# Attention division with heads on partitions, a 128-row projection, and the second biases on GpSimd

## The reference

```
x = x + leaky(sum_e combine_e * (groupnorm(x) @ We_e + be_e))       # 2 of 5 experts
t = tokens(x)                                                       # 16 sequences of 256
q, k, v per head (6 heads of 16), causal softmax(k q / sqrt(96)) v  # -> heads
t = t + heads @ wproj + bproj
w = top-2 softmax weights of (layernorm(t) @ gate_w + gate_b)       # 4 experts, renormalised
t = t + sum_e w_e * (gelu(layernorm(t) @ w1_e + b1_e) @ w2_e + b2_e)
```

## Time and profile before

| what | value |
|---|---|
| median of 3 runs | 353.42 us (352.49 to 353.59) |
| the profiled execution, its own time | 352.74 us |
| span of its trace, first to last instruction | 351.0 us |
| PE busy | 335.9 us, 96% |
| DVE busy | 231.2 us, 66% |
| ACT busy | 231.8 us, 66% |
| POOL busy | 107.8 us, 31% |
| mean granted TensorE clock | 0.988 of full speed |

### The profile page before, as it was taken

How to read it: one execution, slowest core, us unless ns; L and a number is a source line. 1 busy time by engine, 2 the same in 40 slices (tenths; PEclk the granted TensorE clock), 3 DMA queues, 4 the chain that set the end, 5 groups by cost and what they waited for, 6 DMA issues and landing times.

```text
span 351.0 us, 7705 instructions
## 1 busy us (share of the span) xinstructions
PE 335.9 (96%) x2627; PEld 273.5 (78%) x2627; DVE 231.2 (66%) x1025; ACT 231.8 (66%) x467; POOL 107.8 (31%) x179
## 2 busy tenths in 40 slices
PE   6889998879999999999999999999999999999995
PEld 3655466546788987789878988898799789889895
DVE  4859895977379789868686698747647623453232
ACT  3777873555779689548864866497916977374460
POOL 3457761535432224043340434303410305001000
PEclk9999999889999999999999999999999999999999
DMA  7800018452300023013025000500230000000000
GB/s 189 168 4 0 2 35 102 76 63 57 82 3 1 4 67 92 2 52 89 22 69 69 4 23 25 114 5 22 80 57 4 25 2 2 24 1 2 22 2 23
DMA packets 24123, 14.80 MB, mean 42 GB/s; under 512 B 14323, under 2 KB 24083, under 8 KB 24084
## 3 DMA queue, kind: packets, MB, share of 16 engines
q1 hardware_dynamic: 22740, 13.13, 17.0%
q10 hardware_dynamic: 1344, 1.18, 2.7%
HBM read 3.10 MB, written 1.57 MB: 13 GB/s over the span
## 4 chain that ended last, share of the span: by engine, by line
PE 77%; DVE 6%; ACT 6%; DMA 4%; POOL 2%; ACTq 2%; issue 2%; SPq 1%; DVEq 0%; POOLq 0%
PE PS L994 24%; PE PS L787 10%; PE PS L789 9%; PE PS L788 9%; DMA k_stack<-qk_parts 4%; PE PS L931 4%; PE PS L889 3%; PE PS L913 3%; PE PS L840 2%; PE PS L955 2%; PE PS L800 2%; ACTq L684 2%; PE PS L988 2%; PE PS L878 1%; PE PS L940 1%
## 5 line engine op out<-in xcount | busy, mean ns | idle before, releaser
L994 PEld LDWEIGHTS PS<-w_f,hidden 128*128 128x128 f32 x768 | 90.0, 192 | 0.1
L994 PE MATMUL PS<-w_f,hidden 128*128 128x96 f32 x768 | 90.0, 274 | 0.0
L780 ACT ACTIVATE hidden<-PS 128x512 f32<-128x512 f32 x96 | 54.9, 596 | 29.5 <-PE PS L789 27.5
L1234 DVE SCALAR_TENSOR_TENSOR res<-PS,weight,res 128x96 f32<-128x96 f32 x128 | 31.7, 311 | 48.3 <-PE PS L994 48.2
L1152 DVE CUSTOM_DVE_ANT_0 masked<-PS,causal 128x128 bf16<-128x128 f32 (+1 forms) x120 | 35.1, 353 | 9.5 <-PE PS L878 7.4
L787 PE MATMUL PS<-t_hi,w_hi 97*128 97x512 f32 x96 | 40.9, 426 | 0.0
L800 PE MATMUL PS<-ones_b 128*128 128x512 bf16 x153 | 37.0, 391 | 3.4 <-POOL ones_b L518 3.4
L789 PE MATMUL PS<-t_hi,w_lo 97*128 97x512 f32 x96 | 38.1, 397 | 0.0
L788 PE MATMUL PS<-t_lo,w_hi 96*128 96x512 f32 x96 | 38.1, 397 | 0.0
L622 POOL TENSOR_SCALAR_AFFINE_SELECT prob_a<-prob_a 128x768 f32<-128x768 f32 x16 | 13.9, 866 | 65.5 <-ACT prob_a L742 65.5
L1113 DVE SCALAR_TENSOR_TENSOR PS<-conv_y,weight,PS 128x96 f32<-128x96 f32 x128 | 30.3, 315 | 5.1 <-ACT PS L694 5.0
(11 more groups left out here) (170 smaller groups left out, 703.9 us busy)
## 6 DMA issues: line engine op xcount, KB each, us to landing
q_stack<-qk_parts SPq DMA_DIRECT2D x48, 96.0 KB, 3.2
k_stack<-qk_parts SPq DMA_DIRECT2D x36, 96.0 KB, 3.4
out_dram<-res SPq DMA_DIRECT2D x8, 192.0 KB, 2.2
k_stack<-qk_parts ACTq DMA_DIRECT2D x12, 96.0 KB, 5.9
X<-in_x_dram SPq DMA_DIRECT2D x4, 192.0 KB, 2.9
X<-in_x_dram SPq DMA_DIRECT2D x2, 384.0 KB, 5.2
hidden<-in_L_ffn_w_dram SPq DMA_DIRECT2D x1, 576.0 KB
w_f<-in_L_ffn_w_dram SPq DMA_DIRECT2D x1, 576.0 KB
```

Of the source, the lines that this page charges most:

```text
L780: act.activation(hidden[:, m, 0:T * P], PS[:, bank("ffn1", n, index), 0:T * P], ACT.Gelu).then_inc(act_emptied["ffn1"], 1)
L994: mm = pe.matmul(PS[:, y, t * C:(t + 1) * C], hidden[:, m, t * P:(t + 1) * P], w2_f[:, m, :], start=False, stop=t == T - 1 and c == CHUNKS ...
L1234: ins = dve.scalar_tensor_tensor(res2[:, t, :], PS[:, y, t * C:(t + 1) * C], weight1[:, t, e:e + 1], res2[:, t, :], ALU.mult, ALU.add).the ...
```

## The change

Five things change.

1. The division is done on `pv`'s own layout. DVE copies each head's sum (row 16 of its 32) to all 32 rows of the group with a stream shuffle, takes the reciprocal of the whole tile, and multiplies: for a unit the step `att.0` on 512 columns and `att.1` on 256. The steps `out_t` and `heads_t` and ACT's copies of `pv` and `heads_t` are gone.
2. `proj` multiplies the 128 rows directly, with `wproj` laid out in the same groups of 32 rows, zeros between: each of the four token tiles takes two matmuls, one for the round of four heads and one for the round that holds two heads of each image. The bias sits at row 16 of the first group, where a sum times its reciprocal is one. `pv`'s third list of heads changes so that the shared round is the middle one.
3. The matmuls of `b2` are gone from `ffn2`. POOL has a new step `bias`: for each of the four experts a multiplication of the broadcast bias with the weights (128x384) and an addition into the residual, each waiting for the one before. It starts after `weights` and `norm2`; the first `ffn2` addition of DVE waits for it.
4. The loads change: `wproj` in four strided pieces, `b2` broadcast to 128 partitions, `bproj` to one row; 11 instead of 10.
5. `ORDER` is rewritten throughout, with 152 instead of 153 `warm` matmuls in 19 instead of 15 places.

```diff
     PE: """
-        conv.3@3:2 warm.7@9:6 norm1_t@1:6 warm.17@10:4 conv.0@4:4 conv.1@4:0 conv.2@4:3 v@1:1 qk.0@1:2 qk.1@1:5
+        conv.2@2:6 conv.3@2:0 warm.21@8:2 norm1_t@0:2 warm.3@9:4 conv.0@3:4 conv.1@3:3 conv.2@3:5 qk.0@0:1 qk.1@0:6
...
+        wproj_r = sb("wproj_r", [P, 3, C])
+        b2_rows = sb("b2_rows", [P, E1, C])
+        bias_e = sb("bias_e", [P, TILES, C])
...
+                elif kind == "bias":
+                    weight1, res2 = weight1s[n % WEIGHTS], res2s[n % RES2]
+                    shape = [P, T, C]
+                    if n == 0:
+                        pool.wait_ge(ffn_loaded, 16 * FFN_LOADS)
+                    pool.wait_ge(weight1_ready, n + 1)
+                    pool.wait_ge(normed_ready[1], tile0 + T)
+                    wait_dve(pool, "proj", n)
+                    for e in range(E1):
+                        if n > 0 or e > 0:
+                            pool.wait_ge(bias_added, E1 * n + e)
+                        pool.tensor_tensor(bias_e[:, 0:T, :], b2_rows[:, e, :].unsqueeze(1).to_broadcast(shape),
+                                           weight1[:, 0:T, e].unsqueeze(2).to_broadcast(shape), ALU.mult).then_inc(bias_ready, 1)
+                        pool.wait_ge(bias_ready, E1 * n + e + 1)
+                        pool.tensor_tensor(res2[:, 0:T, :], res2[:, 0:T, :], bias_e[:, 0:T, :], ALU.add).then_inc(bias_added, 1)
...
                             for j in range(HG):
-                                image, h = divmod(HG * r + j, HEADS)
+                                image, h = ((0, j), (j // 2, HG + j % 2), (1, j))[r]
...
-                    wait_act(pe, "heads_t", n)
-                    for t in range(T):
-                        mm = pe.matmul(PS[:, bank("proj", n), t * C:(t + 1) * C], heads_t[:, t * P:(t + 1) * P],
-                                       wproj_f[:, :], start=True, stop=True)
+                    wait_dve(pe, "pv", n, (1,))
+                    for image in range(W):
+                        for half in range(2):
+                            t, rows = 2 * image + half, slice(half * P, (half + 1) * P)
+                            pe.matmul(PS[:, bank("proj", n), t * C:(t + 1) * C], att_t[:, 2 * image, rows], wproj_r[:, 0, :],
+                                      start=True, stop=False)
+                            mm = pe.matmul(PS[:, bank("proj", n), t * C:(t + 1) * C], att_t[:, 1, rows],
+                                           wproj_r[:, 1 + image, :], start=False, stop=True)
...
-                    pe.matmul(PS[:, y, 0:T * C], ones_b[:, :],
-                              b2_parts[:, e * C:(e + 1) * C].unsqueeze(1).to_broadcast([P, T, C]),
-                              start=True, stop=False, skip_group_check=True)
...
+                elif kind == "att":
+                    r = index[0]
+                    rounds = (slice(0, 2), slice(2, ROUNDS))[r]
+                    width = (rounds.stop - rounds.start) * TOKENS
+                    heads = PS[:, bank("pv", n, index), 0:width]
+                    wait_filled(dve, "pv", n, index)
...
+                    step_done(dve.stream_shuffle(sums[:, 0:width], heads, [D] * HS))
                     wait_step()
+                    step_done(dve.reciprocal(sums[:, 0:width], sums[:, 0:width]))
+                    wait_step()
+                    if n > 0:
+                        wait_filled(dve, "proj", n - 1)
+                    dve.tensor_tensor(att_t[:, rounds, :].rearrange("p r t -> p (r t)"), heads, sums[:, 0:width],
+                                      ALU.mult).then_inc(dve_emptied["pv"], 1)
...
                     wait_filled(dve, "ffn2", n, index)
+                    if e == 0:
+                        dve.wait_ge(weight1_ready, n + 1)
+                        dve.wait_ge(bias_added, E1 * (n + 1))
```

More of the change, by code:

```diff
@@ L58 @@
[L58 to L72, removed]
@@ L73 @@
-        ffn1.7@1:3 out_t.0@2:1 out_t.1@2:4 score.1.1@3:5 score.1.2@3:6 score.1.3@3:0 score.1.4@3:3 qk.0@4:2 qk.1@4:1
-        heads_t@2:4 ffn1.8@1:5 ffn1.9@1:6 ffn1.10@1:4 ffn1.11@1:0 ffn2.0@1:5 proj@2:6 shift@3:3 v@4:4 ffn2.1@1:0
-        ffn2.2@1:2 prob.0.0@3:1 conv.0@7:5 norm2_t@2:3 ffn2.3@1:4 prob.0.1@3:6 prob.0.2@3:0 prob.0.3@3:1 prob.0.4@3:5
-        norm1_t@5:2 prob.1.0@3:3 prob.1.1@3:6 prob.1.2@3:0 conv.1@7:4 gate2@2:1 prob.1.3@3:5 prob.1.4@3:3
-        score.0.0@4:6 ffn1.0@2:0 ffn1.1@2:5 ffn1.2@2:3 ffn1.3@2:1 qk.0@5:4 qk.1@5:2 ffn1.4@2:6 pv.0@3:0 score.0.1@4:5
@@ L83 @@
-        ffn2.3@2:0 gate2@3:6 norm1_t@6:4 score.1.0@5:3 pv.0@4:5 pv.1@4:2 score.1.1@5:1 ffn1.0@3:0 out_t.0@4:6
-        out_t.1@4:5 ffn1.1@3:4 qk.0@6:2 score.1.2@5:6 score.1.3@5:5 qk.1@6:0 heads_t@4:4 score.1.4@5:3 v@6:2
-        ffn1.2@3:4 ffn1.3@3:0 proj@4:1 ffn2.0@3:2 ffn1.4@3:4 ffn1.5@3:0 ffn1.6@3:6 ffn1.7@3:1 ffn1.8@3:5 ffn2.1@3:4
-        shift@5:2 norm2_t@4:0 ffn1.9@3:3 ffn1.10@3:6 ffn1.11@3:1 ffn2.2@3:5 score.0.0@6:2 prob.0.0@5:4 prob.0.1@5:3
-        norm1_t@7:0 prob.0.2@5:6 prob.0.3@5:1 ffn2.3@3:5 score.0.1@6:2 prob.0.4@5:4 prob.1.0@5:3 prob.1.1@5:6
@@ L98 @@
[L98 to L102 removed]
+        warm.5@0:0 xt@0:0 xt@1:1 warm.3@1:2 xt@2:2 gavg.0@0:3 xt@3:4 warm.1@2:5 gavg.1@0 xt@4:5 xt@5:6 xt@6:0
@@ new lines @@
+        prob.0.3@1:1 score.0.1@2:3 score.0.2@2:5 score.0.3@2:2 prob.0.4@1:0 prob.1.0@1:6 prob.1.1@1:1 prob.1.2@1:4
+        score.0.4@2:3 score.1.0@2:0 score.1.1@2:5 prob.1.3@1:6 prob.1.4@1:1 score.1.2@2:4 score.1.3@2:2 score.1.4@2:3
+        warm.1@18:0 norm2_t@0:0 conv.0@5:6 conv.1@5:1 conv.2@5:5 pv.0@1:6 pv.1@1:0 gate2@0:1 conv.3@5:4 ffn1.0@0:5
+        ffn1.1@0:2 ffn1.2@0:3 ffn1.3@0:6 ffn1.4@0:0 ffn1.5@0:4 proj@1:1 shift@2:5 norm1_t@3:2 ffn1.6@0:3 ffn1.7@0:6
+        ffn1.8@0:5 ffn1.9@0:0 ffn1.10@0:4 ffn1.11@0:1 prob.0.0@2:3 prob.0.1@2:6 qk.0@3:2 qk.1@3:5 ffn2.0@0:0
@@ L157 @@
[L157 to L160 removed]
+        gstat@0 gstat@1 gmean@0 gstat@2 gvar@0 gstat@3 w_conv@0 gmean@1 gstat@4 gvar@1 gstat@5 gstat@6 gstat@7 gmean@2
```

300 lines of the change are left out of this document (124 added, 176 removed).

## The result

The changed kernel takes 392.78 us, the median of 4 runs (392.17 to 393.99), against 352.96 us for the kernel before beside it: a ratio of 1.114, interval 1.1117 to 1.1163. Medians here are of all executions of a kernel, while ratios leave out the slow ones, those over 1.5% longer than its fastest (one of four in `e6_spare_reciprocals`, two of four in `e9_reciprocals_in_pieces`). The prediction was 357, with a range of 344 to 364. The sign was right and the size was not: 40 us are lost, where 4 were forecast. The profiled execution has a span of 392.0 us against 351.0, and the mean granted clock of TensorE falls from 0.988 to 0.933.

What follows compares the result with a forecast made beforehand. PE was taken to bound the kernel behind `proj@0`, a chain of waits ahead of it. Start 91.2, PE 250.2, end 3.6, waits 7.7 and 2 gave 354.7; plus 1.7 and 0.7, a median of 357, range 344 to 364.

Steps and rivals of the forecast that it cites:

- What PE gains: PE's work: 0.85 us saved a unit, 5.8 us behind the start of `proj@0`, leaving 250.2 us there.
- The bias part: Bias matmuls dropped from `ffn2` on PE: 0.17 us each, four a unit, 0.68 us a unit saved.
- What DVE pays: Division on DVE: 6.8 us a unit instead of 1.17, bounds 3.5 and 7.3, with reciprocals of 2.87 and 1.52.
- The estimate of 370: Reciprocal at eight cycles a column, read from a skill page: 2.3 us more a unit, time near 370.
- PE's waits: PE waiting at `proj` for DVE's division chain in units 1 to 7: 7.7 us in all.
- all other waits: Waits from a nearly full DVE, for a score tile's PSUM bank or a low part of `norm_t`: 2 us, possibly 8.
- The clock: PE from `proj@0` on was taken at the full 2.4 GHz; the sum had no term for a slower clock.
- The start: Up to unit 0's `proj`: `pv.0@0` at 83 instead of 85.85, `proj@0` at 91.2 against 93.00.
- The reordering of `prob` before unit 1's scores: Seven of unit 0's `prob` tiles no longer wait for unit 1's DMA: worth up to 4 us at 77.45.
- POOL's biases: Bias additions on POOL: about 7.6 us a unit, 61 in all, costed at nothing since POOL has room.
- The fast reciprocal: Rival: DVE's reciprocal runs at about 1 ns a column, PE itself sets `proj@0`, time 345; chance 0.20.
- POOL's waits: Rival: POOL's late `weights` and `bias` hold up inverse roots and masks, 2 us in three places, time 363; chance 0.10.

Runs made afterwards that it cites:

- e6_spare_reciprocals: Kernel before, with two extra reciprocals (512 and 256 columns) on a spare tile behind each unit's division, results unused: 388.56 us, ratio 1.0993.
- e9_reciprocals_in_pieces: Kernel before, with six extra 128-column reciprocals on a spare tile in each unit, behind six different DVE steps: 365.7 us, ratio 1.03.
- e7_reciprocals_behind: Changed kernel with maxima replacing the division's reciprocals, and both real reciprocals placed behind the unit's last multiplication, results unused: 386.74 us, ratio 1.0986.
- e4_warm_in_waits: Changed kernel with 92 `warm` matmuls put into nine of PE's waits behind `pv`: 382.34 us, ratio 1.0844.
- e1_no_divide: Changed kernel with each full-width reciprocal replaced by a maximum of the tile with itself, orders and waits kept: 352.0 us, ratio 0.9992.

## Why the prediction was wrong

*What PE gains.* 250.2 us behind `proj@0` were predicted, and the same order at the full clock takes 251.7. That is near, but the 250.2 start from 254.4, in which 0.8 us are idle; from the 253.6 of busy time 4.2 us were to be saved, and 2.0 were. The bias part is right: the biases alone gave 5.9 us of less busy time, against 5.4 priced (8 x 0.68).

*What DVE pays.* The reciprocal was forecast at 2.87 and 1.52 us and took 3.35 and 1.75, above even the upper bounds of 3.2 and 1.7: the fixed part that I took off the short rows was too large. Shuffle and multiplications came as priced (0.74 and 0.69 against 0.68). The chain in unit 7, from the shuffle at 342.02 to the end of the multiplication at 349.70, is 7.7 us against 6.8. Put to the waits as I counted them, 0.9 us more in each of seven units would have made 6 us at the most. It is a term of the wrong size, and not the reason. Two runs say the same: over the maxima 2.4 us a unit cost 23 us and 3.5 cost 41, so the 2.8 us that the forecast's own 2.87 and 1.52 leave would by these two points have cost about 30 (an estimate), and the time would have been near 380 with the reciprocal exactly as priced.

The Trainium skill, VectorE: DVE Perf Modes, section "Walkthrough: the 8-slice pipeline in each mode", gives the reciprocal's divide a repeat count of 8. Read as eight cycles for a column at the page's 0.96 GHz, that is 8.3 ns. The trace has 6.25, which is six such cycles. The estimate of 370 that I drew from it lies nearer the result than my forecast, for a reason that it doesn't contain.

*PE's waits.* The waits at `proj` were right. "0.4, 0.9, 0, 0.6, 2.1, 1.1 and 2.6: 7.7 us" became 0 in units 1 to 4 (in 1, 2 and 4 a wait for `pv`'s bank stands ahead of it) and 3.06, 1.95 and 3.57 in units 5 to 7: each of the last three is its forecast with the 0.9 us by which the chain got longer. What failed is the step behind it, which puts all other waits at 2 us ("I add 2 us; it could be 8") and the clock at nothing. Measured against the terms of the sum, span for span (392.0 against 354.7):

- the start, 91.2 against 96.4: 5.2 us;
- PE's work, 250.2 against 251.7: 1.5 us;
- waits at `proj` behind `proj@0`, 7.7 against 8.6: 0.9 us;
- all other waits behind `proj@0`, 2 against 11.3: 9.3 us;
- the clock, not in the sum: 20.4 us.

Together 37.3. Of the 11.3, 10.8 are waits for the bank that `pv` filled. I had not looked for them, though the diff shows that DVE now reads `pv` where ACT had copied it away; ACT's copies I "cost at nothing". The reason for which I had added the 2 us, a DVE so full that score tiles and low parts come late, makes 0.2 us of waits in the changed kernel. It stands behind the others and comes out when they go: with the reciprocals out of the chain but still in the row (`e7_reciprocals_behind`) 6 of 41 us come back, or somewhat more without its maxima, and in `e6_spare_reciprocals`, where only the row is longer, 35 are lost. How much of the whole is chain, bank or row stays open, since the waits hide one another.

*The clock.* The stretch up to 93 us, the one with waits in it, stood at 0.96, the others at 1.00, and the prediction makes nothing of it. That a wait of 2 us in the middle makes what comes behind it slower wasn't in the sum. It is the largest of the five parts, and at least half of it (10 us) is shown by `e4_warm_in_waits` to be a loss of its own.

*The start.* `proj@0` at 96.4, outside the 88 to 95 that I named. `pv.0@0` began at 86.97, not 83: PE waited 2.9 us for the shift's DMA ahead of the first `prob` tile, which starts at 77.69 and not earlier than before (77.45). The later `pv.0@0` makes 4.0 of the 5.2 us, the way from there to `proj@0`, with its longer chain, the rest. The reordering of `prob` before unit 1's scores gained nothing: in `e1_no_divide` too the first `prob` tile starts at 77.65 and `pv.0@0` at 86.07, against 85.85 before, and its `proj@0` at 91.49 is earlier only by the shorter way behind `pv.0@0`.

*POOL's biases.* Right, at nothing: 7 to 8 us are lost without them. An addition took 1.01 and a multiplication 0.85 us, for 0.91 priced.

*The rivals.* The fast reciprocal (345, 0.20) is out, and `e1_no_divide` shows that even then it would have been 352, so the side of "faster" had too much. POOL's waits are out. The chance of 0.58 for slower was on the right side, though it rested on the waits at `proj`, a small part of the loss; the range had no room for the rest, since three terms (bank, row, clock) were put at 2 us together.
